# Nine early expert tiles, and the expert stage's room split by when its former users are done

## The reference

```
q, k = sigmoid(x Wq + bq), sigmoid(x Wk + bk);  v = x Wv + bv         # 16 heads of 16
# running sums over the sequence give every position of q, k and v a weight
a = causal_linear_attention(weighted q, k, weighted v) @ Wo + bo
h = layernorm(x + a) * g1 + be1
y = layernorm(h + gelu(h W1 + b1) W2 + b2) * g2 + be2
x = layernorm(x + y)
e = argmax(x router_w^T)                       # one expert of 8 for each row
o = square(relu(x fc[e])) pj[e]                # 256 -> 1024 -> 256
out = layernorm(x + o)
```

## Time and profile before

| | |
|---|---|
| median of the timed runs | 870.26 us (868.93 to 872.49) |
| span of the profiled execution, first to last instruction | 866.9 us |
| TensorE busy | 814.9 us (94%) |
| VectorE, GpSimd, ScalarE busy | 583.2, 304.6, 274.3 us |
| moved by DMA | 110.6 MB |

### The profile page before, as it was taken

How to read it: one execution, slowest core, us unless ns; L and a number is a source line. 1 busy time by engine, 2 the same in 40 slices (tenths; PEclk the granted TensorE clock), 3 DMA queues, 4 the chain that set the end, 5 groups by cost and what they waited for, 6 DMA issues and landing times.

```text
span 866.9 us, 19476 instructions
## 1 busy us (share of the span) xinstructions
PE 814.9 (94%) x6910; PEld 655.9 (76%) x6911; DVE 583.2 (67%) x1359; ACT 274.3 (32%) x550; POOL 304.6 (35%) x425
## 2 busy tenths in 40 slices
PE   7879899999999999999999898779999999999995
PEld 3457677678677677677677676668999999999994
DVE  7988878888888988888988847636344444444442
ACT  2324223434434434434434233321222222222220
POOL 8211431414714615615615633634122222222222
PEclk9999999999999999999999899979999999999998
DMA  8999995101001001000000001975555555554540
GB/s 255 280 310 317 307 310 144 49 1 51 25 2 51 26 2 50 25 2 26 26 2 26 26 2 44 371 248 178 203 174 175 175 178 180 177 183 175 178 152 1
DMA packets 69718, 110.59 MB, mean 128 GB/s; under 512 B 5261, under 2 KB 54287, under 8 KB 69648
## 3 DMA queue, kind: packets, MB, share of 16 engines
q1 hardware_dynamic: 66240, 101.17, 37.3%
q0 software_dynamic: 3408, 8.46, 2.6%
HBM read 66.94 MB, written 43.58 MB: 128 GB/s over the span
## 4 chain that ended last, share of the span: by engine, by line
PE 90%; DVE 4%; ACT 3%; issue 2%; DMA 0%; POOL 0%; POOLq 0%; SPq 0%; DVEq 0%; ACTq 0%
PE bank L845 16%; PE bank L856 16%; PE bank L767 7%; PE bank L735 7%; PE bank L778 7%; PE bank L747 7%; PE bank L545 5%; PE bank L697 4%; PE bank L713 4%; PE bank L661 4%; PE bank L554 2%; PE bank L689 2%; PE bank L583 2%; PE bank L575 1%; PE bank L830 1%
## 5 line engine op out<-in xcount | busy, mean ns | idle before, releaser
L1141 POOL TENSOR_TENSOR rstd<-vare,minus_half 128x1 f32<-128x1 f32 x96 | 55.7, 582 | 271.2 <-DVE vare L1406 270.8
L845 PEld LDWEIGHTS bank<-xsT,fc 128*128 128x128 f32 x1248 | 147.8, 195 | 3.8 <-issue 2.1
L845 PE MATMUL bank<-xsT,fc 128*128 128x128 f32 x1248 | 148.5, 278 | 1.4 <-ACT xsT L1020 0.7
L1027 ACT ACTIVATE relu<-bank 128x512 f32<-128x512 f32 x78 | 46.4, 597 | 207.6 <-PE bank L845 207.6
L856 PE MATMUL bank<-pj,act 128*128 x416 | 94.2, 380 | 1.0 <-issue 1.0
L1397 DVE TENSOR_TENSOR sm<-bank,upto 128x512 f32<-128x512 f32 x128 | 79.3, 682 | 19.9 <-PE bank L661 19.9
L856 PEld LDWEIGHTS bank<-pj,act 128*128 128x128 f32 x416 | 77.0, 190 | 10.6 <-issue 1.2
L1196 POOL TENSOR_TENSOR mrstd<-mvare,minus_half 128x1 f32<-128x1 f32 x39 | 22.1, 568 | 163.8 <-DVE mvare L1585 163.8
L767 PE MATMUL bank<-n1T,w1s 128*128 128x256 f32 x256 | 69.4, 395 | 3.2 <-ACT hT L996 2.2
L735 PE MATMUL bank<-n1T,w1s 128*128 128x256 f32 x256 | 67.5, 386 | 2.9 <-ACT hT L979 2.4
L778 PE MATMUL bank<-w2s,hT 128*128 128x256 f32 x256 | 66.2, 387 | 1.5 <-ACT hT L996 1.3
(11 more groups left out here) (236 smaller groups left out, 1455.2 us busy)
## 6 DMA issues: line engine op xcount, KB each, us to landing
fc<-in_fc SPq DMA_DIRECT2D x39, 1024.0 KB, 5.0
routed_rows<-empty SPq DMA_DIRECT2D x64, 520.0 KB, 9.9
pj<-in_pj SPq DMA_DIRECT2D x8, 1024.0 KB, 14.0
xs<-routed_rows SPq DMA_DIRECT2D x39, 130.0 KB, 2.0
x<-in_x SPq DMA_DIRECT2D x8, 512.0 KB, 3.7
xT<-in_xT SPq DMA_DIRECT2D x7, 512.0 KB, 4.8
w1s<-in_w SPq DMA_DIRECT2D x1, 1024.0 KB, 8.0
w2s<-in_w SPq DMA_DIRECT2D x1, 1024.0 KB, 8.9
```

What stands on the lines that cost most here:

```text
L845: last = nc.tensor.matmul(h_bank[n][:, chunk(f)], fc[:, s, k, chunk(4 * n + f)], xsT[:, k, :], start=(k == 0), stop=(k == KT - 1))
L1027: nc.scalar.activation(relu[:, n], src[:], ACT.Relu).then_inc(M["relu"].sem, 1)
L1141: nc.gpsimd.tensor_tensor(rstd[:, n, c], vare[:, n, c], minus_half[:], ALU.pow)\
```

## The change

`EARLY` goes from 6 to 9, so the late tiles go from 33 to 30. The SBUF of the attention is laid out anew: first what is done with the last group's scaled keys (`kp`), in the place that `xs`, `fc` and the small expert tiles take later; then what the pairs and the attention output of the last group use, in the place of `pj`; and what is used longer behind all of that. `wo` has a tile of its own, `parity` moves out of the shared room, and two unused tiles fill the borders. SP's waits follow: rows and up weights of tiles 0 to 2 wait for the last `kp`, the down weights for the last attention output (`wo`) and state (`st`). The LAST tables of all four engines are rewritten; of each only the first lines are shown.

```diff
-EARLY, EARLY_GROUP = 6, 4
+EARLY, EARLY_GROUP = 9, 4
+EARLY_ROOM, DOWN_ROOM = 512, 2784
...
 PE_LAST = [
-    ("b_turn", 7, 0), ("b_turn", 7, 1), ("b_up", 7, 0), ("b_down", 7, 0), ("b_up", 7, 1), ("b_down", 7, 1),
+    ("b_turn", 7, 0), ("m_turn", 0, 0), ("b_turn", 7, 1), ("d_count", 5, 0), ("b_up", 7, 0), ("b_up", 7, 1),
...
 DVE_LAST = [
-    ("m_finish", 4, 0),
+    ("m_finish", 4, 0), ("m_square", 6, 0), ("m_finish", 5, 0), ("m_square", 7, 0), ("m_finish", 6, 0),
+    ("m_finish", 7, 0), ("m_square", 8, 0),
...
-            ev["h1b"].wait(sp, G - 1, NC)
+            ev["kp"].wait(sp, G - 1, KT)
+            sp.wait_ge(spare_in, 16)
+            for g in range(G):
+                sp.wait_ge(gone[g], 16 * E)
             sp.wait_ge(rt, R_EARLY)
...
             for s in range(3):
                 load_rows(0, s, early[s][1])
                 load_up(0, s, early[s][0])
+            early = [(of_tile(expert, j, E - 1), of_tile(at_tile, j, E * NT)) for j in range(3, 6)]
+            ev["wo"].wait(sp, G - 1, NC)
+            ev["st"].wait(sp, G - 1, NC)
             for e in range(E):
                 load_expert(e)
-            early = [(of_tile(expert, j, E - 1), of_tile(at_tile, j, E * NT)) for j in range(3, 6)]
-            for s in range(3):
-                load_up(1, s, early[s][0])
-                load_rows(1, s, early[s][1])
+            for t in range(1, EARLY // 3):
+                for s in range(3):
+                    load_up(t, s, early[s][0])
+                    load_rows(t, s, early[s][1])
+                if t + 1 < EARLY // 3:
+                    early = [(of_tile(expert, j, E - 1), of_tile(at_tile, j, E * NT)) for j in range(t * 3 + 3, t * 3 + 6)]
```

More of the change, by code:

```diff
@@ L32 @@
 NO_TOKEN = 1 << 20
-EARLY, EARLY_GROUP = 6, 4
+EARLY, EARLY_GROUP = 9, 4
+assert EARLY * P <= (EARLY_GROUP + 1) * T - E * (P - 1)
 LATE = SLOTS - EARLY
 LAST_PERIODS = G + 1
+EARLY_ROOM, DOWN_ROOM = 512, 2784
 class Event:
@@ L186 @@
 POOL_LAST = [
[3 rows of a table removed]
-    ("d_count", 6, 0), ("m_store", 0, 0), ("m_store", 1, 0), ("d_count", 7, 0), ("m_store", 2, 0), ("m_store", 3, 0),
-    ("m_store", 4, 0), ("m_store", 5, 0),
[3 rows of a table added]
+    ("m_store", 0, 0), ("d_count", 6, 0), ("m_store", 1, 0), ("d_count", 7, 0), ("m_store", 2, 0), ("m_store", 3, 0),
+    ("m_store", 4, 0), ("m_store", 5, 0), ("m_store", 6, 0), ("m_store", 7, 0), ("m_store", 8, 0),
 ]
@@ L234, in build @@
         unread = sb("unread", [P, 1])
+        parity = sb("parity", [P, 2])
         early, early_i = sb("early", [P, E]), sb("early_i", [P, E], I32)
@@ L271, in s1 @@
             return sb(name, shape, dt, part1)
-        wqkvo = s1("wqkvo", [P, 4, KT, D])
+        wqkv = s1("wqkv", [P, 3, KT, D])
         bq, bk = s1("bqs", [P, KT]), s1("bks", [P, KT])
-        bv, bo, g1, be1 = (s1(n, [P, D]) for n in ("bvs", "bos", "g1s", "be1s"))
+        bv = s1("bvs", [P, D])
         head_of = s1("head_of", [P, HPT])
@@ L294, in build @@
         total_ex = s1("total_ex", [P, L // T])
+        empty = s1("empty", [P, ROW])
+        in_block = s1("in_block", [P, 4])
+        residue, chunk_of = s1("residue", [P, HPT]), s1("chunk_of", [P, NC])
+        spare_room = s1("spare_room", [P, EARLY_ROOM])
+        kT = s1("kT", [P, 2, KT, T])
+        qs = s1("qs", [P, KT, T])
         vpad = s1("vpad", [P, 2, NC, H // 2, 4 * DH])
-        parity = s1("parity", [P, 2])
         qm = s1("qm", [P, 2, KT, T])
@@ L302, in build @@
         xat = s1("xat", [P, 2, KT, P])
+        wo_s = s1("wo", [P, KT, D])
+        bo = s1("bos", [P, D])
+        down_room = s1("down_room", [P, DOWN_ROOM])
+        g1, be1 = s1("g1s", [P, D]), s1("be1s", [P, D])
         xb = s1("xb", [P, NC, D])
         r1, hg = s1("r1", [P, NC, D]), s1("hg", [P, 2, D])
-        empty = s1("empty", [P, ROW])
-        in_block = s1("in_block", [P, 4])
-        residue, chunk_of = s1("residue", [P, HPT]), s1("chunk_of", [P, NC])
         begin_room = hg[:].rearrange("p c d -> p (c d)")
@@ L408, in load_w @@
             def load_w(n, done):
-                sp.dma_start(wqkvo[:, n], wqkvo_d[n].rearrange("(k p) n -> p k n", p=P)).then_inc(done, 16)
+                tile = wo_s[:] if n == 3 else wqkv[:, n]
+                sp.dma_start(tile, wqkvo_d[n].rearrange("(k p) n -> p k n", p=P)).then_inc(done, 16)
             def load_rows_of(tile, src, done):
@@ L499, in _ @@
             for s in range(2):
-                load_up(2, s, late[s])
+                load_up(EARLY // 3, s, late[s])
             sp.wait_ge(rt, R_DONE)
             late_rows = [of_tile(at_tile, EARLY + s, E * NT) for s in range(3)]
-            sp.wait_ge(spare_in, 16)
             for half in range(2):
                 sp.wait_ge(scattered[half], 16 * NT // 2)
-            load_rows(2, 0, late_rows[0])
-            load_rows(2, 1, late_rows[1])
-            load_up(2, 2, late[2])
-            load_rows(2, 2, late_rows[2])
-            with sp.Fori(3, SLOTS // 3) as t:
+            load_rows(EARLY // 3, 0, late_rows[0])
+            load_rows(EARLY // 3, 1, late_rows[1])
+            load_up(EARLY // 3, 2, late[2])
+            load_rows(EARLY // 3, 2, late_rows[2])
+            with sp.Fori(EARLY // 3 + 1, SLOTS // 3) as t:
                 for s in range(3):
@@ L519, in _ @@
         def _(pe):
-            wq, wk, wv, wo = (wqkvo[:, n] for n in range(4))
+            wq, wk, wv = (wqkv[:, n] for n in range(3))
+            wo = wo_s[:]
             def project(g, half, n):
@@ L881, in _ @@
             pe.wait_ge(rt, R_EXPERT)
-            turn_rows(2, 0)
+            turn_rows(EARLY // 3, 0)
             def three_tiles(t, last):
@@ L896, in three_tiles @@
                 return before
-            three_tiles(2, False)
-            with pe.Fori(3, SLOTS // 3 - 1) as t:
+            three_tiles(EARLY // 3, False)
+            with pe.Fori(EARLY // 3 + 1, SLOTS // 3 - 1) as t:
                 three_tiles(t, False)
```

42 lines of the change are left out of this document (21 added, 21 removed), and 12 rows, old and new, of tables (DVE_LAST, POOL_LAST).

## The result

The changed kernel takes 866.01 us (median of 20 runs, 863.49 to 871.79), the kernel before 871.42 us beside it (20 runs): ratio 0.9939, 95% interval 0.992 to 0.9958. That is 0.6% faster, and 1.4 us above the forecast of 864.6 us. The profiled execution took 864.4 us with a span of 862.6 us, 4.3 us less than before.

A forecast was written before the change was run, and what follows sets the result against it. TensorE's unbroken late-tile matmuls bound the kernel, so only their start could move. Terms -8.8 (A and B), 0, -1.6, +3.0, +1.7 sum to -5.7 us: span 861.2 us, plus 3.4 us for timed runs, 864.6 us; range 859 to 870 us.

The forecast's parts named there:

- A: Stretch up to the first expert up: reordered FFN and earlier group 6 rows start it at 553.3 us, 5.0 us gained.
- B: Up of tile 0 to up of tile 1: the latter starts at 560.5 us, -8.8 us together with A.
- C: TensorE's clock in up of tile 1: falls again, the up takes 6.11 us as before, 0 change.
- D: End of up of tile 1 to up of tile 6: 36.2 us instead of 37.8 us, -1.6 us.
- E: End of early tiles: TensorE stops before tile 9 for VectorE's finish 7 and square, +3.0 us; lower clock behind it, +1.7 us.
- Loads: Earlier expert rows and weights: credited with nothing by themselves, bounds 0 to 1.05 us; nobody waits at the first down.
- The first (the clock holds): Rival: clock stays up before tile 1, or also before tile 9, giving 862.1 or 860.4 us; chance 0.25.
- the second (rows of group 6 no earlier): Rival: collisions and ScalarE waits leave tile 0 at 557 to 558.4 us, time 868.3 to 869.7 us; chance 0.21.
- The third: Rival: row 0 of group 7 waits for group 5's scatter, starting late and landing slowly, up to 873.7 us; chance 0.09.

The follow-up runs named there:

- three edits: Changed kernel with VectorE squaring tile 8 before finishing tile 7, GpSimd adding be2 for group 7 early, and expert numbers read before each up: 859.88 us, ratio 0.9879.
- square first: Changed kernel with one pair exchanged on VectorE, the square of tile 8 ahead of the finish of tile 7: 863.51 us, ratio 0.9911.
- own rows: Changed kernel with down weights held until the last h1b, plus a separate buffer for rows 0 and 1 of group 7: ratio 0.9944 to the kernel before.
- early addition: Changed kernel with GpSimd's addition of be2 for group 7 moved ahead of its last mean of the first norm: ratio 0.9948 to the kernel before.

## Why the prediction was right, and where it was not

The working reached the end by the path that it named, with one price missing (that of the loads) and misses that cancel in part. On the chain of waits, against the profile before:

| step | forecast | measured |
|---|---|---|
| A + B, up of tile 1 (569.33 before) | -8.8 | -8.7 (560.61) |
| C, that up | 0 | -0.9 (5.25 us, not 6.11) |
| D, its end to up of tile 6 | -1.6 | 0 (37.85 us, not 37.84) |
| E, the stop, with up 6 to 8 | +3.0 | +3.7 (25.71 us, not 21.97) |
| E, the clock | +1.7 | +1.9 (5.44 us, not 3.57) |
| sum | -5.7 | -4.0; span -4.3 |

The 0.3 us between the sum and the span were not traced. That the median came within 1.4 us of the forecast is luck in part: C came out 0.9 us better, D 1.6 us and E 0.9 us worse, and the executions of the changed kernel alone span 8 us. By the prediction's own bound, faster below 865.9 us, 866.01 us stands on the edge, though the interval of the ratio is clear of 1.

**A and B** hold, in place and size, and taking the FFN order back gives most of A back. In A the collision was of the larger size. GpSimd's addition held the placing for 1.2 us, where the row before showed 0.6. That is what the Trainium skill ("SBUF — State Buffer", section "Who interferes with whom") states, an exclusive lock for the whole instruction; the trace agrees to 0.06 us (541.49 against 541.55). The row before fits it too: its operation began only 0.8 us before the addition's end (547.69 against 548.50 us), so it could not be held longer. Up of tile 0 was in time all the same, because 0.5 us had been set aside.

One reading behind B was wrong. The 2.42 us of idleness at 562.5 us were put down to row 0 of group 7. That row was done at 562.96 us, and the chain has 1.99 us more until its turn, with no releaser. The turn also waits for VectorE's sum of group 6's counts, whose end, 564.85 us, is 0.1 us before it:

```profile
564.69 0.16 DVE L1498 TENSOR_TENSOR acc<-bank,acc 128x8 f32<-128x8 f32 x1
```

The new order moved that sum too (it ends at 558.26 us, before row 0), so the forecast of B came out; its old value was read as a time, and needed no cause.

**C** was mis-sized: the clock fell, but not for the whole up.

**D** was the mis-sized term. 31.58 us of the 37.85 are four ups and five downs; for the rest I had 4.65 us and 6.27 came. Restarts behind a turn or a wait cost 1.24 us, not 0.5; the logits 1.66, not 1.3; turns and counting, with short gaps between them, 1.91, not 1.7; the expert number 0.72, not 0.8. The last piece was 0.74 us, not 0.35: a wait of 0.34 us for the rows of tile 5, and 0.41 us before the down behind them, which is gone in the three edits, where the expert number is read earlier. The table of the late tiles is at the root of the first, as forecast, but by another way than the square of tile 3. It holds up VectorE's residual of tile 2; in the chain the load of the rows follows that residual and takes 2.90 us:

```profile
588.60 2.90 DMA xs<-routed_rows
591.51 0.04 issue
591.55 0.44 PE bank L851 x2
591.99 0.41 issue
592.40 3.72 PE bank L877 x16
```

**E** holds: its release, its length (3.28 us for 3.2) and its clock; square first removed it. What the 3.0 us lacked is 0.3 us in the stop, and the same restarts in tiles 6 and 7, 7.55 and 7.63 us and not 7.25.

**Loads.** "I credit the earlier loads with nothing by themselves" is the step that failed, though the time did not show it, since A to E were worked out with the weights in place. The bound of 1.05 us was read at the old place of the first down (577.50 + 1.05 us, 45.7 us behind the first turn); the change brings that down to 33.3 us behind the turn, so with all loads late it stands until the last weight has landed, and the stretch is 9.8 us longer (339.8 against 330.0), more than the whole gain. With the down weights alone late no down waits, and the stretch is still 4.2 us longer (334.14 against 329.96). I had looked only at who waits for the weights, and had left out who shares the DMA engines with them. In the profile before the same scatter ran beside the same loads without a wait, since row 0 came later there.

**Rivals.** The first (the clock holds) and the second (rows of group 6 no earlier) did not occur in the profile after. The third has a real mechanism, which the late down weights and the run with own rows show; its trigger is the landing, not the issue.

**Open.** That the scatter lands late because the DMA engines are full is read from their shares in the runs with late weights (1.07 against 0.43); no run changed that share alone. Why the lower clock falls in one profile and not in another stays open, and with it 1.7 us in every stretch.

## What to carry to other kernels

Price an earlier load at the place that its reader will have, and by everyone who is on the DMA engines at the old time: here they had cost at most 1.05 us of waiting at the old place, and putting all of them back cost 9.8 us. When work is added to a hand-written order, look at the last piece's release: three more tiles cost 5 us through one line of VectorE's table. And read an expected gain against a stretch that the edit leaves alone, if the front of the program moves by itself.

## What the runs showed of the hardware

Two things I had not expected. The unchanged part up to the first turn of group 7 differs by up to 7 us between profiles, with the granted clock of the first 100 us: 0.98 in the changed kernel's profile, 0.93 in that of the early addition.

```profile
0.00:100.00 100.00, 84.14 (x698) 55.08 (x700) 82.87 (x138) 33.60 (x58) 37.10 (x73) 0.98 1.00 294
```

```profile
0.00:100.00 100.00, 84.16 (x679) 54.64 (x681) 78.86 (x136) 32.76 (x56) 33.08 (x71) 0.93 0.99 289
```

Over the 20 runs of the changed kernel time and granted clock go together (correlation -0.87; 863.49 us at 0.990, 871.79 us at 0.978). And much the same idle stretches before up of tile 1 lowered its clock in one profile and not in another: 0.87 and 0.90 us with an up of 5.41 us in the changed kernel, 0.80 and 0.90 us with one of 5.41 us in the run with the square first, 0.83 and 0.90 us with one of 3.74 us in the run with own rows. So the length of these stretches alone does not decide it.
